# A vision tower of five layers: a new order of work in its first attention, and the tokenizer's squares issued one group earlier

## What is computed

```python
h = tokenizer(x)                  # 5 shifted copies, 36 patches per image, layernorm over 3840, project to 192
h = h + attn0(layernorm(h))       # 12 heads of 16, softmax, output projection: "phase B"
h = h + ffn0(layernorm(h))        # 12 heads of 64 with normed q and k, gated heads: "phase C"
h = h + attn1(layernorm(h))       # 12 heads of 64, q and k scaled: "phase D"
h = h + ffn1(layernorm(h))        # 192 -> 3072 (768 kept by a top-k mask) -> 192: "phase E"
```

```python
q, k, v = split(xh @ W_qkv[h] + b_qkv[h])        # xh: 16 features of the head
p = softmax(q @ k.T / sqrt(192))                 # 36 x 36 per image
out = concat_heads(p @ v) @ W_out + b_out
```

## Time and profile before

| | us |
|---|---|
| median of 3 runs (range) | 1408.65 (1405.73 to 1414.64) |
| the profiled execution | 1416.0 |
| its span, first to last instruction | 1413.6 |
| tokenizer's last second moment | at 107.4 |
| phase B, first scores to last residual | 115.6 to 349.9 |

### The profile page before, as it was taken

How to read it: one execution, slowest core, us unless ns; L and a number is a source line. 1 busy time by engine, 2 the same in 40 slices (tenths; PEclk the granted TensorE clock), 3 DMA queues, 4 the chain that set the end, 5 groups by cost and what they waited for, 6 DMA issues and landing times.

```text
span 1413.6 us, 26944 instructions
## 1 busy us (share of the span) xinstructions
PE 1208.1 (85%) x9226; PEld 1105.6 (78%) x9226; DVE 944.5 (67%) x2350; ACT 884.6 (63%) x3172; POOL 438.3 (31%) x467
## 2 busy tenths in 40 slices
PE   6987777786699999999779999999970059999998
PEld 4877677775589999999669999999850049999998
DVE  4455876655488888888557888888848863333333
ACT  1565787765389999999668989898842012222232
POOL 0001021020333333333043334344314225555555
PEclk9997999998699999999989999999975579999999
DMA  9202002000000000000000000000022000000000
GB/s 372 90 1 68 2 1 68 1 2 1 0 2 1 1 2 2 2 1 2 11 1 1 2 2 2 1 1 2 1 78 79 0 1 1 11 10 8 3 11 13
DMA packets 7857, 30.41 MB, mean 22 GB/s; under 512 B 2094, under 2 KB 4894, under 8 KB 6174
## 3 DMA queue, kind: packets, MB, share of 16 engines
q1 hardware_dynamic: 7724, 28.69, 6.0%
HBM read 26.92 MB, written 1.77 MB: 20 GB/s over the span
## 4 chain that ended last, share of the span: by engine, by line
PE 60%; DVE 9%; ACT 4%; issue 1%; POOL 1%; POOLq 0%; DVEq 0%; ACTq 0%
PE bank L1394 6%; PE bank L1359 6%; PE bank L1325 4%; DVE f_eq L1652 4%; PE bank L1385 4%; PE bank L1345 3%; PE bank L1368 3%; PE bank L1329 3%; PE bank L1326 3%; PE bank L1327 3%; PE bank L1328 3%; PE bank L1731 2%; PE bank L1716 2%; PE bank L1718 2%; PE bank L1717 2%; PE bank L1736 2%
## 5 line engine op out<-in xcount | busy, mean ns | idle before, releaser
L1163 ACT ACTIVATE t_p<-bank,t_nmax 108x108 f32<-108x108 f32 x792 | 266.6, 352 | 29.7 <-DVE t_nmax L713 29.0
L1837 POOL TENSOR_TENSOR f_hid_lo<-f_hid,f_hid_hi 128x432 fp32r<-128x432 f32 (+2 forms) x144 | 145.7, 1013 | 158.7 <-ACT f_hid_hi L1823 158.7
L713 DVE TENSOR_REDUCE t_nmax<-bank 108x4 f32<-108x432 f32 x198 | 119.8, 605 | 111.5 <-PE bank L1359 111.4
L999 POOL TENSOR_TENSOR t_sq<-t_raw 108x768 f32<-108x768 f32 x88 | 141.9, 1612 | 168.9 <-ACT t_raw L1103 168.4
L1359 PE MATMUL bank<-t_kT,t_qT 128*108 128x108 f32 x1584 | 188.8, 263 | 3.9 <-ACT t_p L1163 1.4
L1793 DVE SCALAR_TENSOR_TENSOR f_hid<-bank,f_maskT 128x432 f32<-128x432 f32 (+2 forms) x144 | 80.3, 557 | 163.9 <-PE bank L1720 162.7
L1359 PEld LDWEIGHTS bank<-t_kT,t_qT 128*108 128x108 f32 x1584 | 181.4, 179 | 10.2 <-ACT t_p L1163 8.3
L1823 ACT CAST f_hid_hi<-f_hid 128x432 fp32r<-128x432 f32 (+2 forms) x144 | 73.9, 513 | 179.4 <-DVE f_hid L1793 179.4
L1163 ACT ACTIVATION_READ_ACCUMULATOR t_p<-bank,t_nmax 108x1 f32 x792 | 164.7, 208 | 0.0
L731 DVE TENSOR_TENSOR t_p<-t_p,t_rinv 108x432 f32<-108x432 f32 x198 | 146.0, 737 | 6.8
L1171 ACT COPY t_pT<-bank 108x432 f32<-108x432 f32 x198 | 102.4, 518 | 44.0 <-PE bank L1368 43.0
(11 more groups left out here) (227 smaller groups left out, 3233.2 us busy)
## 6 DMA issues: line engine op xcount, KB each, us to landing
A_x<-in_x SPq DMA_DIRECT2D x5, 1728.0 KB, 18.5
A_w<-in_tok_w SPq DMA_DIRECT2D x5, 768.0 KB, 7.1
f_raw_down<-in_w_proj SPq DMA_DIRECT2D x1, 2304.0 KB, 8.7
out_tokens<-h SPq DMA_DIRECT2D x21, 81.0 KB
f_raw<-in_w_mfc SPq DMA_DIRECT2D x1, 1536.0 KB, 7.5
f_raw<-in_w_mfc SPq DMA_DIRECT2D x2, 768.0 KB, 12.3
W_raw<-in_wC SPq DMA_DIRECT2D x1, 1159.0 KB
W_raw<-in_wC SPq DMA_DIRECT2D x2, 579.5 KB
```

The source lines that it names most:

```text
L713: dve.tensor_reduce(b.nmax[:, 4 * c:4 * c + 4], self.sbank[(3 * g + c) % 2][0:GT, 0:4 * GT].rearrange("p (a n) -> p a n", n=GT), AX.X, ALU ...
L999: pool.tensor_tensor(sq, v, v, ALU.mult).then_inc(s["sq"], 1)
L1163: act.activation(b.p[g % 2][:, m, :], self.sbank[(3 * g + c) % 2][0:GT, n * GT:(n + 1) * GT], ACT.Exp, bias=b.nmax[:, m:m + 1], accum_out= ...
L1837: pool.tensor_tensor(self.hid_lo[m % 4][:, c], self.hid[m % 4][:, c], self.hid_hi[m % 4][:, c].bitcast(F32), ALU.subtract).then_inc(s["lo" ...
```

## The change

In the tokenizer ACT issues three squares first and then `root(n)`, `square(n+3)`; DVE runs `finish(n-1)` ahead of `statistics(n)`; phase B's start-up steps lie at other values of n, and there are more of them (up to the first queries and keys: nine on DVE and ACT instead of seven and six, six on PE instead of three).

In phase B the three loops of PE, DVE and ACT are written again, as loops of 24 turns. Values of group g-2 and its output projection now stand in turn g (before, those of g-1), and the last transpose of group g stands in turn g+1 behind its scores. Queries and keys share bank 1 alone, values have bank 0 alone, and banks 4 and 5 serve x and p. No instruction is added or taken away; phases C, D and E keep their order.

```diff
@@ tokenizer, vector
                 sum_squares(n + 1)
-            statistics(n)
             if n:
                 finish(n - 1)
-
-            if n in (9, 10, 11, 13, 14, 16, 20):
+            statistics(n)
+
+            if n in (4, 5, 6, 8, 9, 10, 15, 17, 19):
                 next(ahead, None)
@@ tokenizer, scalar
-        square(0)
-        square(1)
+        for n in range(3):
+            square(n)
         for n in range(GROUPS):
             root(n)
-            if n + 2 < GROUPS:
-                square(n + 2)
-            if n in (10, 11, 13, 14, 19, 20):
+            if n + 3 < GROUPS:
+                square(n + 3)
+            if n in (6, 7, 9, 10, 13, 14, 17, 18, 20):
                 next(ahead, None)
@@ tokenizer, tensor
-            if n in (18, 19, 20):
+            if n in (12, 13, 16, 17, 18, 20):
                 next(ahead, None)
@@ Attention, banks
-        self.qbank, self.sbank, self.tbank = bank[0:2], bank[2:4], bank[4:6]
+        self.qbank, self.sbank, self.tbank = bank[0:1] if kind == "B" else bank[0:2], bank[2:4], bank[4:6]
+        self.qkbank = bank[1:2] if kind == "B" else None
@@ Attention, vector
+        for g in range(GROUPS + 2) if kind == "B" else ():
+            this, before = g < GROUPS, 0 < g <= GROUPS
+            if this:
+                row_max(g, 0)
+            if before:
+                weigh(g - 1, 2)
+            if g + 1 < GROUPS:
+                spread_q(g + 1)
+            if g + 4 < GROUPS:
+                norm_apply(g + 4)
+            if this:
+                row_max(g, 1)
+                weigh(g, 0)
...
@@ Attention, scalar
+            if this:
+                exps(g, 0)
+            if g >= 2:
+                copy_o(g - 2, 0)
+            if before:
+                copy_p(g - 1, 0)
+            if g + 3 < GROUPS:
+                copy_x(g + 3)
+            if this:
+                exps(g, 1)
...
@@ Attention, tensor
+            if this:
+                scores(g, 0)
+            if g + 1 < GROUPS:
+                turn_qk(g + 1, 0)
+            if before:
+                turn_p(g - 1, 0)
+            if g >= 2:
+                values(g - 2, 0)
+            if g + 3 < GROUPS:
+                turn_x(g + 3)
+            if this:
+                scores(g, 1)
...
@@ Attention, tensor: a user of a bank waits for its last user there
-            self.evacuated(pe, "qk", g, u, before=2)
+            self.evacuated(pe, "qk", g, u, last_user=True)
```

More of the change, by code:

```diff
@@ L937, in vector @@
             gate_step(4)
-            if kind == "B" and more:
-                spread_q(g + 1)
             weigh(g, 0)
@@ L1212, in scalar @@
             norm_root(n + 4)
+            yield
         for u in range(self.qk_act):
@@ L1215, in scalar @@
                 copy_qk(0, u)
+        yield
+        for g in range(GROUPS + 2) if kind == "B" else ():
+            this, before = g < GROUPS, 0 < g <= GROUPS
+            if this:
[9 more added lines that the diff above has]
+            if before:
+                copy_p(g - 1, 1)
+            if g + 1 < GROUPS:
+                copy_qk(g + 1, 1)
+            if g and g + 5 < GROUPS:
+                norm_root(g + 5)
+            if this:
+                exps(g, 2)
+            if before:
+                copy_p(g - 1, 2)
+            if beside:
+                beside(act, g)
+        if kind == "B":
+            return
         for g in range(GROUPS + 1):
             this, before, more = g < GROUPS, g > 0, g + 1 < GROUPS
-            chunks = kind != "B" and g + 2 < GROUPS
+            chunks = g + 2 < GROUPS
             if g + 3 < self.x_turns:
@@ L1239, in scalar @@
                 norm_root(g + 5)
-            if kind != "B" and more:
+            if more:
                 roots(g + 1, 1)
@@ L1249, in scalar @@
                 copy_chunk(g + 2, 3)
-            if kind != "B" and more:
+            if more:
                 copy_qk(g + 1, 1)
-            if before and len(self.pv_split) > 1:
+            if before:
                 copy_o(g - 1, 1)
@@ L1265, in scalar @@
                 roots(g + 2, 0)
-            if before and kind == "B":
-                copy_o(g - 1, 0)
-            if kind == "B" and more:
-                copy_qk(g + 1, 1)
-            if beside:
-                beside(act, g)
         if self.tail:
```

111 lines of the change are left out of this document (80 added, 31 removed).

## The result

The changed kernel takes 1362.67 us (median of 4 runs, 1361.70 to 1366.71) beside 1411.37 for the kernel before on the same chip (4 runs, 1405.73 to 1414.64): a ratio of 0.966, interval 0.962 to 0.971. It is 48.7 us faster by these medians, where 53 were forecast, and the time lies in the range (1356 said, 1340 to 1378). Its profiled execution has a span of 1359.5 us, against 1413.6.

The account below looks back on a forecast made before the run. Rings of waits, no full engine, were taken to bound tokenizer and phase B. Phase B's 197.2 us from 96.5 ended 56.2 us sooner, 19 from the tokenizer; less 3 for clock, 1408.65 - 53 = 1356 us, range 1340 to 1378.

Parts of the forecast that it names:

- PE as the bound and 2.81 us a group: Tokenizer: with squares three ahead, PE sets the pace, 2.81 us a group instead of 3.54.
- Term 1: Tokenizer and phase B's start-up: first scores at 96.5 instead of 115.6, 19 us gained; bounds 10 and 20 us.
- Rings walked at 7.60 and 7.59: Phase B, undisturbed group: two loops of dependent work through PE, DVE and ACT; 7.8 us taken, against 10.25 before.
- The 0.2 added for PE's restart: Phase B: PE restarts slower after a wait, so 0.2 us raises the group to 7.8 us.
- the rule that speaks for two banks: Phase B: skill's PSUM bank rotation; keys sharing the queries' bank would wait for `spread_q`, 1386 us; rival's chance 0.10.
- Weight preparation: Phase B: DVE steps and ACT casts lose their cover, 18.7 us given back; bounds 5 and 25.
- The price of a step (1.6): Phase B: each DVE-only preparation step delays the row maximum by 1.6 us; four groups counted.
- The sum for phase B: Phase B, first scores to last residual: turns, preparation and both ends make 197.2 us, from 96.5 to 293.7.
- the 30.3 said: Phase B's ends: first two groups 14 us, chain from the last group's first scores 16.3 us.
- the rival that had it at half throughout: Phase B: PE's clock falls to 1.2 GHz, a group takes 14.4 us, time 1473 us; chance 0.02.
- The 3 us allowed for stretches at 1.2 GHz: Phase B: 3 us taken off the gain for slow-clock stretches that could not be placed.
- The lower rival: Phase B: PE at its floor of 7.22 us, preparation half absorbed, 1342 us; lower edge of the forecast's 0.80.

Follow-up runs that it names:

- `pair_banks`: Changed kernel with the old banks: queries and keys back on banks 4 and 5 with x and probabilities, values over 0 and 1; 1381.57 us, ratio 0.977.
- `finish_late`: Changed kernel with `statistics(n)` put ahead of `finish(n-1)` again in the tokenizer, three squares ahead kept; 1361.39 us, ratio 0.965.
- `pool_split`: Changed kernel with each of POOL's five subtractions for the weights' low parts cut into four column pieces; 1359.93 us, ratio 0.962.
- `best_twelve`: Changed kernel with DVE's preparation steps halved, ACT's roundings quartered, raw weights sooner, first scores awaiting 21 finishes, POOL's subtractions in twelve pieces; 1337.61 us, ratio 0.948.

## Why the prediction was right, point by point

- **Tokenizer.** PE as the bound and 2.81 us a group: right. The last moment came at 96.4 instead of 94.7. Group 3's passes started at 38.33 instead of 37.62, which is 0.7 of it. PE waited 0.98 us at 85.91 for `values_in` to empty the only bank left to values; the start-up needs the single bank twice in a row. In `pair_banks`, with two banks, this stretch is 1.1 us shorter (56.98 against 58.11). `finish(n-1)` ahead of `statistics(n)` was said to help PE's bank; `finish_late` shows that it does nothing for the pace.
- **First scores.** The step that failed here is "Now only the copy of the first keys is left behind the last piece, some 1.0 us". It is the last finish that is left, with the moment, the statistics (behind the finish of the group ahead) and the root ahead of it, 2.75 us from the last moment. Term 1 came to 16.4 us instead of 19.
- **An undisturbed turn.** Rings walked at 7.60 and 7.59, 7.67 measured. The 0.2 added for PE's restart was hardly needed: the step was right by rows and its surcharge wrong. Nineteen turns at 7.67 are 2.5 us less than at 7.8. It also lies under the 7.9 us that PE's busy time by matmuls would have given as a floor, and over the 7.22 of its weight loads.
- **Banks.** Keys wait for `spread_q` in no turn but the first ones (0.7 us in all). The walk was right against the rule that speaks for two banks, which would have made it 1386. `pair_banks` adds that two banks in common with other work cost 1.1 us a turn.
- **Weight preparation.** The mechanism was right and the term undersized. The eleven longer turns hold 110.5 us, 26.2 more than at 7.66, against 18.7. By comparison with the same turns in the other runs they divide, as an estimate, into some 10 us of DVE steps, 10.7 of roundings, 3.3 of `weigh` standing still for POOL and 2.3 of the clock. The price of a step (1.6) was right, but it was put at four of the six steps only: the two in turns that also have a rounding were left out, and they cost about as much (9.50, the turn with the second of them, is 1.8 over 7.67). The roundings cost 2.0 to 2.2 where nothing else is in the turn, and less in two of the six. The standstill was missing altogether: 14.8 us over phase B, of which about 3.3 reached the last residual. The prediction took POOL only for a possible late comer.
- **The sum for phase B.** Forecast 197.2, measured 200.1 (99.19 to 299.33): preparation +7.5, the turns -2.5, and the first and last turns some 2 less than the 30.3 said, in spite of 1.4 us of half clock behind the last group's scores. With +2.7 at the first scores the end lies 5.6 us behind the forecast 293.7.
- **The clock.** It was granted at 0.97 over the last 160 us of phase B, so the rival that had it at half throughout was wrong. The 3 us allowed for stretches at 1.2 GHz, which the prediction could not place, were about right: there were three, of 3.4 us each, and they cost 1.7, 0.6 and 1.4 us.
- **Wait of PE for `copy_p` at the second transpose**: right in place. Waits for `copy_p` ahead of transposes are the most of PE's waiting in phase B, 23.3 us in 19 waits. In an undisturbed turn it is 0.16 us and PE is full, 37.65 us of loads in 40.
- **The lower rival.** Its terms don't give its time: 1356 less 11 us for turns at 7.22 and less 9 for half the preparation is 1336, not 1342. Nothing measured hangs on it, but the range's lower end does.

In the profiled executions the gain is 54.3 us (1416.0 to 1361.70) where 53 were forecast, and part of that nearness is luck. Phase B ended 50.6 us sooner instead of the 53.2 that the sum had after its 3 us for the clock: the barrier not read (2.7), the two steps left out (3.6, with a small surplus of the others) and the collision of two engines (3.3) were mostly made up by the surcharge (2.5), by cheaper roundings (1.6) and by the first and last turns (some 3.5 without their part of the clock). The later phases then gave 3.5 us that no term had. By medians the gain is 48.7, 4 us short, but the median before is taken from four runs between 1405.73 and 1414.64 us, so those 4 us can't be put down to any one cause.

## What to carry to other kernels

When a timetable is tightened, small work that used to lie in waits is no longer free: cut it into pieces about as long as a wait that is left, and put each into one. Ask of every long instruction beside the ring what it shares with the engines in the ring. An all-SBUF tensor_tensor on DVE beside a long one on POOL stands still until that ends, so cut POOL's work short rather than adding to it. Behind a ring's end, list every wait of the first instruction of the next stage, the barriers among them, and not only the data that it reads. When two executions are compared turn by turn, look at the granted clock of each turn first: here a stretch of 3.4 us at half the full clock cost up to 1.8 us.

## What was not expected of the hardware

- A DVE tensor_tensor of SBUF operands (0.61 us) held up by one on POOL (5.1 us) to within 0.47 us of POOL's end, five times in phase B: 3.01, 2.99, 3.90, 4.05 and 4.03 us. Reductions out of PSUM, reciprocals and a tensor_scalar with one tensor in SBUF were not held up.
- Cutting POOL's subtraction of 2318 columns in four costs it 16% (5.09 to 5.90 us), in twelve about 50 to 80% (7.5 to 9.1 us, with DVE at work beside it). Phase B's turns still got shorter: by 3.3 us in all with four pieces instead of one (`pool_split`), and by 2.8 with twelve instead of four (`best_twelve`).
- PE's turn ran at 7.67 us with two waits of 0.16 and 0.17 us in it, where weight loads alone take 7.22: little more than 0.1 us was lost otherwise.
- In the unchanged phases C, D and E, whose instructions are the same, executions differ by up to 4.4 us (1060.2 to 1064.6); the shortest three are those with PE's clock at 0.94, all others have 0.93.
